# Transformer block on one core: normalization one slot earlier, feed-forward row work elsewhere in VectorE's turn, loads in other slots

## The reference

```python
h = _layernorm(x, ln1_g, ln1_b)
x = _attention(h, h, sa_wq, sa_wk, sa_wv, sa_wo, sa_bo) + x
h = _layernorm(x, ln2_g, ln2_b)
x = _attention(h, cond_emb, ca_wq, ca_wk, ca_wv, ca_wo, ca_bo) + x
h = _layernorm(x, ln3_g, ln3_b)
p = h @ ff_w1 + ff_b1
a, gate = (p[..., :D_FF], p[..., D_FF:])
h = a * jax.nn.gelu(gate, approximate=False) @ ff_w2 + ff_b2
return h + x
```

## Time and profile before

| | us |
|---|---|
| median of 3 runs | 1696.74 |
| lowest, highest | 1695.99, 1697.89 |
| the profiled execution's own time | 1697.57 |
| its span, first to last instruction | 1695.8 |

### The profile page before, as it was taken

The page is one execution under the profiler, slowest core; times in us unless marked ns, Lnnn a source line. Parts: engine busy times, 40 slices in busy tenths (PEclk is TensorE's granted clock), DMA queues, the critical chain, the costliest instruction groups (busy, mean ns, idle before and its releaser), DMA issues.

```text
span 1695.8 us, 39063 instructions
## 1 busy us (share of the span) xinstructions
PE 1680.5 (99%) x11712; PEld 1560.7 (92%) x11712; DVE 1396.4 (82%) x2964; ACT 1247.5 (74%) x3379; POOL 1079.5 (64%) x1804
## 2 busy tenths in 40 slices
PE   8999999999999999999999999999999999999999
PEld 8999999999999999999999999999999998888888
DVE  8887888888888888889888888888888877656665
ACT  7788788888888888888888888888888886122221
POOL 7776577777766666787777777777777565231211
PEclk9999999999999999999999999999999999999999
DMA  7776677778766567887787878787776785212110
GB/s 214 183 180 161 171 208 190 204 198 211 196 176 159 153 167 200 230 222 185 190 209 196 205 196 210 193 210 182 197 177 176 192 211 139 69 50 72 64 40 26
DMA packets 301138, 288.91 MB, mean 170 GB/s; under 512 B 103425, under 2 KB 252033, under 8 KB 300929
## 3 DMA queue, kind: packets, MB, share of 16 engines
q1 hardware_dynamic: 247136, 273.29, 61.8%
q10 hardware_dynamic: 53792, 13.12, 3.5%
HBM read 82.98 MB, written 37.49 MB: 71 GB/s over the span
## 4 chain that ended last, share of the span: by engine, by line
PE 89%; DVE 3%; SPq 3%; issue 2%; POOL 1%; DMA 1%; ACT 1%; ACTq 0%; DVEq 0%; POOLq 0%
PE QKB L556 16%; PE PVB L638 13%; PE PTB L569 11%; PE WOP L620 10%; PE VB L491 8%; PE S L458 6%; PE S L459 6%; PE S L1282 5%; PE PTB L1282 5%; PE QKB L1304 3%; PE VB L1304 3%; PE QKB L538 2%; SPq L673 1%; SPq L675 1%; SPq L1616 1%
## 5 line engine op out<-in xcount | busy, mean ns | idle before, releaser
L780 ACT ACTIVATE PT<-S,NM 128x256 f32<-128x256 f32 x1024 | 471.9, 473 | 147.2 <-DVE NM L945 146.0
L889 DVE TENSOR_TENSOR PL<-PTB,PH 128x512 fp32r<-128x512 f32 x512 | 350.9, 686 | 128.2 <-ACT PH L813 127.9
L1143 POOL TENSOR_TENSOR ON<-ON,RB 128x256 f32<-128x256 f32 x256 | 188.1, 735 | 287.4 <-DVE ON L965 265.5
L945 DVE TENSOR_REDUCE NM<-S 128x2 f32<-128x512 f32 x512 | 327.3, 681 | 0.3
L813 ACT ACTIVATE PH<-PTB 128x1024 fp32r<-128x1024 f32 x256 | 264.3, 1032 | 67.9 <-PE PTB L569 66.3
L569 PE MATMUL PTB<-IDN,PT 128*128 128x128 f32 x2048 | 265.7, 273 | 0.1
L458 PE MATMUL S<-RX 128*128 128x256 f32 x1012 | 253.9, 283 | 0.8 <-DMA RX<-QKS 0.8
L459 PE MATMUL S<-RX 128*128 128x256 f32 x1012 | 253.7, 283 | 0.0
L556 PE MATMUL QKB<-HT,WQ 128*128 128x512 f32 x936 | 242.9, 394 | 0.9
L620 PEld LDWEIGHTS WOP<-WO,OT 128*128 128x128 f32 x1536 | 217.5, 190 | 20.1 <-POOL OT L1148 0.2
L569 PEld LDWEIGHTS PTB<-IDN,PT 128*128 128x128 f32 x2048 | 229.5, 140 | 1.1 <-issue 0.5
(11 more groups left out here) (163 smaller groups left out, 2918.7 us busy)
## 6 DMA issues: line engine op xcount, KB each, us to landing
RX<-QKS SPq DMA_DIRECT2D x506, 192.0 KB, 2.9
RX<-QKS SPq DMA_DIRECT2D x506, 128.0 KB, 2.8
RB<-denominators SPq DMA_DIRECT2D x512, 64.0 KB, 2.7
out_dram<-XR SPq DMA_DIRECT2D x32, 256.0 KB, 3.5
weights_qk<-SPL SPq DMA_DIRECT2D x32, 256.0 KB, 3.4
WQ<-weights_qk SPq DMA_DIRECT2D x32, 256.0 KB, 3.4
rows<-XN SPq DMA_DIRECT2D x24, 256.0 KB, 2.6
rows<-HF SPq DMA_DIRECT2D x23, 256.0 KB, 2.7
```

The costliest lines, as they stand in the source:

```text
L780: last = e.activation(PT[:, c % 2, j * S:(j + 1) * S], S1[:, i, qt * S:(qt + 1) * S], ACT.Exp, bias=NM[:, j:j + 1], accum_out=DEN[:, c % 2 ...
L889: e.tensor_tensor(PL[:, cols], PTB[:, i, :], PH[:, s % 2, cols].bitcast(F32), ALU.subtract).then_inc(a.dve_pl, 1)
L945: e.tensor_reduce(NM[:, i * TT:(i + 1) * TT], S1[:, i, :].rearrange("p (t s) -> p t s", t=TT), AX.X, ALU.max, negate=True).then_inc(a.dve_ ...
```

## The change

- `normalized_in(c)`: sequences 6 to 15 are normalized at start_of(n)-2 instead of -1; all others stay.
- The feed-forward row work of VectorE in the attention slots moves from the end of its slot into `dve_ffn_rows`, called right behind `dve_rows`. Chunk 1's statistics are taken in slots 244 to 246, its normalization comes to slots 249 to 252, behind a wait for chunk 0's low parts; GpSimd's RSTD for it comes at slot 247, behind a wait for chunk 0's normalization. SyncE stores the rows in slots 251 and 253; raw copies 4 and 5 (into XN and HF) wait for those stores.
- In the feed-forward, chunk 1's turns stand in steps 3 and 4, ScalarE's rounding in step 4; its row loads wait for the second product (`dve_hf` 2).
- The early copies of value tiles wait for GpSimd's tile v-4 instead of v-1.
- TensorE does gates(5) ahead of second(1).
- SyncE: the bias load moves from slot 248 to 237; loads of WV from 120 to 119, 128 to 129, 248 to 247 and 256 to 257; the last two quarter loads of WQ from 254 and 255 to 255 and 256.

```diff
+def normalized_in(c):
+
+    n = due(c, -2, 2)
+    if n and OLD // PAIRS + 2 <= n < B:
+        return n
+    n = due(c, -1, 2)
+    return None if n and OLD // PAIRS + 2 <= n < B else n
...
-            if due(c, -1, 2):
-                e.wait_ge(a.dve_th, due(c, -1) - 1)
-                dve_normalize(e, sl, a, due(c, -1), (near(due(c, -1)),))
+            n = normalized_in(c)
+            if n:
+                e.wait_ge(a.dve_th, n - 1)
+                dve_normalize(e, sl, a, n, (near(n),))
...
+        def dve_ffn_rows(e, c):
+
+            if c == FFN_START - 16:
+                e.wait_ge(a.dve_xo, B + HOLD + 2)
+                dve_stats(e, zero_ffn, fs, 0, 0, 1)
+            if c == FFN_START - 15:
+                dve_stats(e, zero_ffn, fs, 0, 2, 3)
+            if c == FFN_START - 14:
+                dve_aggregate(e, zero_ffn, fs, 0)
+            if c == FFN_START - 12:
+                e.wait_ge(a.s_ht, 4 * B)
+                e.wait_ge(a.pl_ct, 2 * B)
+            if FFN_START - 12 <= c < FFN_START - 8:
+                dve_normalize(e, zero_ffn, fs, 0, ROWS, (c - FFN_START + 12,))
+            if FFN_START - 6 <= c < FFN_START - 4:
+                dve_ffn_turn(e, 0, c - FFN_START + 6)
+            if c == ATT - 12:
+                e.wait_ge(a.dve_xo, B + HOLD + 4)
+                dve_stats(e, zero_ffn, fs, 1, 0, 1)
+            if c == ATT - 11:
+                dve_stats(e, zero_ffn, fs, 1, 2, 3)
+            if c == ATT - 10:
+                dve_aggregate(e, zero_ffn, fs, 1)
+            if c == ATT - 7:
+                e.wait_ge(fs.s_ht, KD)
+            if ATT - 7 <= c < ATT - 3:
+                dve_normalize(e, zero_ffn, fs, 1, ROWS, (c - ATT + 7,))
...
-                sl.wait(e, a.pl_v, v)
+                sl.wait(e, a.pl_v, v - 3)
...
             dve_rows(e, sl)
+            dve_ffn_rows(e, c)
...
+            if n in (4, 5):
+                e.wait_ge(d_fs[n - 4], 16 * 2)
...
+                if chunk == 1:
+                    e.wait_ge(fs.dve_hf, 2)
...
-            if c >= 0 and c % PAIRS == 6 and sl.has(c + PAIRS):
+            if c >= 0 and c % PAIRS == (6 if c >= PAIRS else 4) and sl.has(c + PAIRS):
...
-                if f == (2 if chunk else 3):
+                if f == 2 and chunk:
                     sl.wait(e, fs.s_ht, KD * (chunk + 1))
                     dve_normalize(e, sl, fs, chunk + 1, ROWS)
-                turn = f - (4 if chunk else 5)
+                turn = f - (4 if chunk else 3)
...
-            if sl.c == ATT - 3:
+            if sl.c == ATT - 9:
+                e.wait_ge(fs.dve_xn, 2)
                 pool_rstd(e, zero_ffn, fs, 1)
...
                             at = LAST + 4 * (quarter - 2)
+                            turns = ((0, 1, 2, 3), (0, 1, 3, 4))[quarter - 2]
...
-                            if c == at + chunk:
+                            if c == at + turns[chunk]:
...
-                            if c == four + 2 + 2 * n:
+                            if c == four + 2 + (n if g == 0 else 3 * n):
...
-                if c == ATT - PAIRS:
+                if c == ATT - 19:
                     e.wait_ge(a.pl_xb, 2 * B)
                     e.dma_start(BOUT[:, :], ff_b2.partition_broadcast(P)).then_inc(d_bo, 16)
...
+                if c in (ATT - 5, ATT - 3):
+                    store_ffn_rows(1, (c - ATT + 5) // 2)
...
                 if chunk + 1 < NCK:
-                    store_ffn_rows(chunk + 1, 0, 1)
+                    if chunk:
+                        store_ffn_rows(chunk + 1, 0, 1)
                     load_ffn_rows(e, chunk + 1, *range(8))
...
+            pe_gates(e, EARLY + 1)
             pe_second(e, 1)
-            pe_gates(e, EARLY + 1)
```

More of the change, by code:

```diff
@@ L1496, in dve_attention_slot @@
                 dve_aggregate(e, sl, a, 1)
[L1497 to L1517, removed]
         def pool_low(e, *ns):
@@ L1690, in fill_weights @@
                             at = j - LEAD + 2
+                            turns = (0, 1, 2, 3)
                         for chunk in range(4):
-                            if c == at + chunk:
+                            if c == at + turns[chunk]:
                                 if chunk == 0:
```

## The result

The changed kernel took 1689.88 us (median of 5, 1687.83 to 1690.59) beside 1696.74 (median of 5, 1695.89 to 1698.22): ratio 0.9953 with a 95% interval of 0.9942 to 0.9964, faster by 6.9 us. Forecast were 1688.4 in 1685.5 to 1692.5. Its profiled execution took 1689.88 with a span of 1688.1, which is 7.7 less than the old span of 1695.8; the sum of the steps had been 8.35.

The account below looks back on a forecast made before the run. TensorE, busy 99% of the span, was taken as the bound, so only its gaps could go. Six terms summed to 8.35 us off the profiled 1697.57, giving 1689.2; the median being 0.83 lower, 1688.4 was forecast, range 1685.5 to 1692.5.

Parts of the forecast that it names:

- C: Late attention: chunk 0's row work moved ahead of the reciprocal closes five gaps of TensorE; 0.9 us (0.3 to 1.2).
- D: SyncE's bias and weight loads moved: the ring copy TensorE waits for in slot 251 leaves sooner; 0.95 us (0 to 0.96).
- E: Chunk 1's statistics moved from slots 250-252 to 244-246: the excess in slot 253 goes; 0.5 us (0 to 1.2).
- F: Changeover to feed-forward: gates(5) ahead of second(1), gates(6) and gates(8) start sooner; 2.2 us (0 to 4).
- A: Self phase: normalization of sequences 6 to 15 a slot sooner, nine slots at 0.35; 3.15 us.
- Rival (a): Self phase: VectorE and GpSimd collide in the new slot, so A gives only 0.4; 1691.2 us, 10%.
- Rival (e): Self phase: something else, such as the residual addition, makes the split late, so A is nil; 1691.6 us, 3%.
- B: Start: value copies no longer wait for GpSimd's previous tile, VectorE goes on sooner; 0.65 us (0 to 0.98).
- a sixth, in slot 240: Late attention: a gap beside the five in C, said to follow from a late ScalarE and to stay.
- rival (b): Late attention: queues become the bound, ring copies land no sooner, C, D and E give 0.3; 1690.5 us, 12%.
- Rival (c): Changeover: turn 1 or the passes ahead of gelu(5) come 2 us later, F gives nothing; 1690.6 us, 8%.
- Rival (d): Changeover: chunk 1's row loads land late and TensorE stands at gates(7), kernel slower; 1700.7 us, 2%.

Follow-up runs that it names:

- the repeat: The changed kernel run again unaltered, in the rounds of later runs: 1689.12 us (median of 5), ratio 0.9952.

## Why the prediction was right, and where its steps were off

At equal clock the change is worth 1696.37 - 1688.96 = 7.4 us (standard error 0.3), against 8.35 forecast. The range and the direction were right, and most of the mechanism; that the number came this near is in part luck, since C was forecast too small, D, E and F too large.

The difference of the two profiled executions, 7.7, holds things that are no term of the change. The old one was 1.2 above its kernel's mean at full clock, and two things account for most of that: its late start (0.35 in slot 2 and about 0.2 before), which no later trace has, and the gap of slot 127 (0.52), which comes and goes (whole in one later trace, smaller in three, absent in nine). Against them stands the fall of the clock in the new one (0.69). The prediction's sum held neither; but it took the whole 8.35 off the median. Its 1688.4 is 1.5 below the first median and 0.7 below the repeat's 1689.12.

- **A right**: 3.15 forecast, 3.22 in the trace, 3.60 by the means at full clock (1696.37 - 1692.77). Rival (a), the collision with GpSimd, is out: all nine steps gave 0.35 to 0.37. Rival (e) is out with it.
- **B right**: 0.65 forecast, 0.79 in the trace, 0.72 by the means at full clock (give or take 0.3).
- **C mis-sized**: 0.9 forecast. Against the 75.13 us of slots 232 to 246 with the row work moved, the three traces without have 1.84, 1.53 and 0.63 more, 1.3 on average. The step that was off is "a sixth, in slot 240, follows from a late ScalarE and stays": with the row work moved it is absent in all eleven traces. That ScalarE was late there was right, though, and one trace without the edit lacks the gap too. The 0.3 that the prediction took off for ring copies belongs to the next term.
- **D and E mis-sized together**: 1.45 forecast. The wait of slot 251 (0.96 with its slow matmuls) went in all ten traces of the new order, and the excess of slot 253 (0.65) as said, but ring copies were waited for again, 1.06 on average and about 0.17 of slow matmuls behind them, mostly three or four slots later: about 0.4 is left. The step that failed is that the second store "may take 0.2 back"; the prediction's own sign of being wrong, a DMA wait near slots 245 or 255, came. Moving the stores did not mend it. Nor is the bias load shown to be what made the wait of slot 251, as D had it: the run with only the rows placed kept that load and had no wait. So rival (b) was half right.
- **F mis-sized**: 2.2 forecast, 23.91 - 22.31 = 1.60 at full clock from outputs(253) to gates(8), and 0.91 in the trace with the fall. The failed step is "waits for outputs(255), about 1440.5: L1412 ends at 1442.0". 1440.5 is the start of outputs(255), and its six matmuls take 0.98, so L1412 stays where it was behind it: from outputs(255) to gates(6) it is 2.55 us in both kernels. VectorE's normalization was not on this path. So gates(6) came 0.53 sooner, not 1.0: the 0.60 us wait of second(1) went, and one of 0.29 for GpSimd's OT came ahead of outputs(255). The rest of the chain held: passes ahead of gelu(5), the wait at gates(7) (0.33 for 0.65), none at gates(8). Rival (c) is out.
- **The fall of the clock** was in no term. It costs about 1.6 us where nothing hides it (4.61 against 3.01 at gates(8)), and 0.69 net in the changed kernel, whose slow gates(6) covers the wait at gates(7).
- Rival (d), row loads late, did not come up: ScalarE rounds chunk 1 from 1437.86 on, right behind VectorE's turns.

The terms as measured, 3.22 + 0.79 + 1.3 + 0.4 + 1.6 = 7.3, stand against 7.4 by the means.

## What to carry to other kernels

Before a gap is booked as a term, ask whether it is the kernel's or that one execution's. Later traces of kernels that left these places as they were put the wait for a ring copy anywhere from 0 to 1.44 us, and one of them lacks the gaps of slots 240 and 241; more profiles of the old kernel could have shown as much beforehand. A wait that sits beside a suspicious transfer need not be that transfer's; here the issuing queue had 0.2 to 0.4 us to spare in a slot, so that a long issue some slots earlier may be the one that lands there. In a chain, add from the end of an operation, not its start, and look first for work that stands behind a wait it doesn't need, as step 4 did behind the last residual addition: that was worth as much as the whole of F.

## What the runs showed of the hardware

- TensorE's granted clock fell to 0.50, its 1.2 GHz level, behind single waits of 1.57 or 1.82 us in a kernel that keeps it busy 99% of the time. Five traces show the fall; by the mean clock 48 of 113 executions of kernels with such a wait had one and the others had none. Matmuls of 128x512 then took 628 ns as a rule and up to 797 in the trace with the stores on ScalarE, instead of 389 as the profile has them. The Trainium skill (TensorE: Matmul & The Clock Gate, "Part 1: The HAM clock gate") has the clock at half or full and nothing between; the trace agrees, since its values of 0.61 and 0.73 are windows with both.
- SyncE's issue of a transfer, 0.6 us as a rule, took 0.9 to 2.3 us now and then late in attention (mostly 11 to 23 us apart), on whichever transfer was next. The longest waits for ring copies stand in traces with much of this, but not in all such traces.
